# Layer-0 values by token, silu in one ScalarE operation, norm constants on VectorE, reordered loads, and a new order of the stages

## The chip, the cores and the metric

One core of one Trainium2 chip. The metric is the device time of one execution in microseconds; lower is better. The time before is the median of 3 runs.

## What is computed

The input x has 32 sequences of 32 tokens with 128 features. Two layers follow each other:

```python
# layer 0: a conditioned transformer block, 16 heads of 8 channels
cmod = silu(c) @ w_ada + b_ada                  # six vectors of 128 for each sequence
x_mod = ln(x) * (1 + scale_msa) + shift_msa
k, q, v = split(x_mod @ w_qkv, 3)
w = softmax((q / 8) @ k.T)                      # for each head, 32 x 32
x = x + gate_msa * ((w @ v) @ w_proj + b_proj)
h = gelu((ln(x) * (1 + scale_mlp) + shift_mlp) @ w_mlp1 + b_mlp1)
x = x + gate_mlp * (h @ w_mlp2 + b_mlp2)
# layer 1: graph attention in two directions d, over the first 20 tokens
self = concat(x, q or 0) @ W_self.T + b_self    # 0 where a row of x sums to 0
out = self
for d in (0, 1):
    vb = A[d] @ w_bias + b_bias                 # A: the int32 mask, or its transpose
    w = softmax(where(A[d].sum(-1) > 0, qd @ kd.T / sqrt(8), NEG) + vb)
    out = out + (w @ self[:20]) @ Wout[d] + bout[d]
x = x + relu(out)
```

## The kernel before, in words

The 1024 tokens are 8 groups of 128 (4 sequences each). TensorE (PE) computes a score unit, one group of one layer and direction, as 16 small matmuls into `ps_s` (`scores`, L699). Heads are split as 4 x 4: V and K are spread over four masked copies (`take k` on ScalarE (ACT) L761; `spread` on ACT L819 for layer 0 and L816 for layer 1). VectorE (DVE) takes the maximum (`max`, L982 or L977), the difference is formed on DVE (L993, layer 0) or GpSimd (POOL, L535, layer 1), PE transposes the result (`turn`, L711), ACT takes the exponential into PT (`exp`, L824), PE multiplies by V (`values`), and DVE divides by the sum (`recip` and `mult`). There are 24 such units, 8 of layer 0 and 16 of layer 1.

Layer 0's values are feature-major before: V is the stationary operand and PT the moving one (L727), so y comes out as features by tokens, ready for the projection. The sums come from a second product with `quad_ones` (L731), four matmuls of 128 columns, and are as wide as y: the reciprocal (L1004) covers 128x128 elements and the product is L1016. Layer 1's values are token-major: PT is stationary and 36 columns of Vz are moving, 32 of V and 4 of ones that give the sums (L736); the reciprocal (L1002) covers 128x16 and the product (L1011) broadcasts it.

At the start, ACT issues the three loads of x (L743); SP issues cols, the first third of w_ada, w_qkv and the rest of w_ada (L438 to L442), waits for x and w_ada, and then issues adj, w_rest and xT (L445 to L447). silu is exp on ACT (L745) and add, reciprocal and product on DVE (L857 to L859); then follow the products with w_ada (`cmod`, L610). The norm of layer 0 works in the chunks of `STARTS` (1, 2, 2 and 3 groups): `stats` on DVE (L838, L841), `rstd` on POOL (L463 to L476: variance plus epsilon, minus the mean, the power, and the product of the two), `apply` on DVE (L846) for chunk 0 and on ACT (L804) for the others, a transposition (`xnT`, L584), two takes on DVE (L895, L893), and then the products q, k and v (L622). From the projection (L630) on the work goes in `PIECES` of 2, 3 and 3 groups: proj, x1tok (transposed for the second norm), xn2T, four mlp1 (L640) and mlp2 (L645), then rowsum, self, q1, k1 and v1 of layer 1. `label` operations on POOL (L510 to L530) reduce the mask to the bias of layer 1.

One list, `ORDER`, written out by hand, sets the order of the stages on all engines: each engine goes through it and issues the instructions of its own stages in that order. An instruction that waits holds all that stand behind it on its engine. `BANKS` says which of four PSUM banks each product uses; PE waits until the bank's last product has been taken. `fill` stages and `WARM` are matmuls of the identity whose results nobody reads.

## Time and profile before

| | |
|---|---|
| median of 3 runs | 95.74 us (95.59 to 96.35) |
| profiled execution, its own time | 95.43 us |
| its span, first to last instruction | 93.6 us |
| instructions | 4637 |
| PE, DVE busy | 88%, 79% of the span |
| ACT, POOL busy | 67%, 68% of the span |
| TensorE clock granted | 1.00 throughout |

Busy time is the union of an engine's instructions. The execution's own time is 1.8 us longer than the span; that part lies around it. PEld is the loading of weights, which overlaps the matmuls. In the rows, x32 counts instruction records; an f32 product has two of them.

### The profile page before, as it was taken

The page shows a single profiled execution, that of the slowest core. Times are in us where ns is not written, and L with a number is a line of the kernel's source. Part 1 is how long each engine was busy: PE and PEld are TensorE (multiplying, and loading weights), DVE is VectorE, ACT ScalarE, POOL GpSimd, SP SyncE. Part 2 cuts the span into 40 slices and gives each one's busy share as a digit, 9 for nine tenths or more (in the row PEclk, how much of TensorE's full clock was granted, in tenths as well). Part 3 has the DMA queues.
Part 4 walks back from the last instruction along what each step waited for, and adds up shares of the span by engine and source line. Part 5 has one row for each costly group of instructions (what it writes and reads, how often), then busy time and mean ns, then how long its engine had stood idle before and what let it go on. Part 6 is the DMA issues. An engine that isn't in the chain of part 4 may idle for free.

```text
span 93.6 us, 4637 instructions
## 1 busy us (share of the span) xinstructions
PE 82.8 (88%) x1904; PEld 57.5 (61%) x1904; DVE 73.7 (79%) x209; ACT 63.1 (67%) x129; POOL 63.3 (68%) x117
## 2 busy tenths in 40 slices
PE   3998999977985998899998999999999999997920
PEld 3996646735653685558564676558476775776810
DVE  2598798999999879994089998746399748969990
ACT  0707999966892387338970669999954547899720
POOL 6967489995599129999655199049807399895400
PEclk9999999999999999999999999999999999999999
DMA  1939994000000000000000000000000000000033
GB/s 37 304 148 308 419 399 196 0 10 3 7 0 7 0 0 3 7 0 0 0 7 0 0 7 0 7 0 7 0 7 3 7 0 7 7 3 7 7 112 112
DMA packets 2532, 5.04 MB, mean 54 GB/s; under 512 B 336, under 2 KB 1872, under 8 KB 2256
## 3 DMA queue, kind: packets, MB, share of 16 engines
q1 hardware_dynamic: 2080, 4.23, 12.5%
q10 hardware_dynamic: 432, 0.52, 1.6%
q8 instruction: 15, 0.25, 1.0%
q14 instruction: 5, 0.04, 0.1%
HBM read 4.23 MB, written 0.52 MB: 51 GB/s over the span
## 4 chain that ended last, share of the span: by engine, by line
PE 57%; DVE 26%; issue 7%; POOL 5%; ACT 1%; DVEq 0%; POOLq 0%; ACTq 0%
PE ps_p L640 8%; PE ps_p L645 7%; PE ps_s L699 7%; PE ps_p L711 7%; DVE rden_T L1004 6%; POOL Kb L550 4%; DVE neg_max L982 4%; PE ps_s L570 4%; PE ps_p L736 3%; PE ps_p L584 3%; DVE E L993 3%; PE ps_p L665 2%; PE ps_p L570 2%; DVE tok L1021 2%; PE ps_p L654 2%
## 5 line engine op out<-in xcount | busy, mean ns | idle before, releaser
L824 ACT ACTIVATE PT<-ps_p 128x512 f32<-128x512 f32 x24 | 14.0, 598 | 5.4 <-PE ps_p L711 5.1
L535 POOL TENSOR_TENSOR E<-E,neg_max 128x320 f32<-128x320 f32 x16 | 11.5, 726 | 8.6 <-DVE neg_max L977 8.6
L711 PE MATMUL ps_p<-ident,E 128*128 128x128 f32 x96 | 14.6, 278 | 0.3 <-issue 0.3
L550 POOL TENSOR_SCALAR Kb<-k_raw,cols,head_mask 128x240 f32<-128x240 f32 (+1 forms) x24 | 12.1, 518 | 3.8 <-ACT k_raw L779 3.8
L711 PEld LDWEIGHTS ps_p<-ident,E 128*128 128x128 f32 x96 | 10.9, 141 | 2.8 <-issue 1.5
L816 ACT ACTIVATE Vz<-V_turned 20x384 f32<-20x384 f32 (+1 forms) x24 | 11.5, 483 | 0.8 <-DVE V_turned L902 0.2
L766 ACT ACTIVATE hidden<-ps_p,cols 128x384 f32<-128x384 f32 (+1 forms) x12 | 6.1, 544 | 6.5 <-PE ps_p L640 6.3
L640 PE MATMUL ps_p<-xm,w_rest_sb 128*128 128x384 f32 (+1 forms) x24 | 8.7, 470 | 1.0 <-DVE xm L893 0.9
L969 DVE TENSOR_TENSOR E<-ps_s,bias_dir 128x320 f32<-128x320 f32 x16 | 7.7, 479 | 1.8 <-PE ps_s L699 1.8
L819 ACT ACTIVATE Vz<-V_turned,quad_mask 128x256 f32<-128x256 f32 (+2 forms) x16 | 7.8, 522 | 0.0
L736 PEld LDWEIGHTS ps_p<-Vz,PT 128*32 128x32 f32 x512 | 5.7, 111 | 3.2 <-issue 1.5
L1004 DVE RECIPROCAL rden_T<-ps_p 128x128 f32<-128x128 f32 x8 | 7.6, 951 | 0.1
L977 DVE TENSOR_REDUCE neg_max<-E 128x16 f32<-128x320 f32 x16 | 7.5, 475 | 0.2
L736 PE MATMUL ps_p<-Vz,PT 128*32 128x36 f32 x512 | 7.0, 201 | 0.6 <-ACT PT L824 0.6
L645 PE MATMUL ps_p<-hidden,w_rest_sb 128*128 128x384 f32 (+1 forms) x24 | 7.4, 451 | 0.0
L520 POOL TENSOR_TENSOR label_bias<-label_bias,label_tmp 128x256 f32<-128x256 f32 x10 | 7.3, 734 | 0.0
L761 ACT ACTIVATE Kb<-ps_p,head_mask 128x256 f32<-128x256 f32 (+2 forms) x16 | 6.7, 472 | 0.7 <-PE ps_p L622 0.7
L699 PE MATMUL ps_s<-Kb,q1T 32*32 32x80 f32 x512 | 7.1, 240 | 0.1
L622 PE MATMUL ps_p<-xm,w_qkv_sb 128*128 128x256 f32 (+2 forms) x24 | 7.1, 397 | 0.0
L910 DVE SCALAR_TENSOR_TENSOR ps_p<-ps_p,cols,cmod 128x384 f32<-128x384 f32 (+1 forms) x6 | 3.4, 571 | 4.1 <-PE ps_p L645 4.1
L518 POOL TENSOR_TENSOR label_sum<-label_sum,tok 128x256 int32<-128x256 int32 x9 | 6.6, 730 | 0.0
L1002 DVE RECIPROCAL rden<-ps_p 128x16 f32<-128x16 f32 x16 | 3.7, 240 | 3.6 <-PE ps_p L736 3.6
(100 smaller groups left out, 189.5 us busy)
## 6 DMA issues: line engine op xcount, KB each, us to landing
tok<-in_adj SPq DMA_DIRECT2D x1, 1408.0 KB, 5.6
w_rest_sb<-in_w_rest SPq DMA_DIRECT2D x1, 1088.0 KB, 7.9
xT<-in_xT SPq DMA_DIRECT2D x1, 512.0 KB, 8.7
x_tok<-in_x_tok ACTq DMA_DIRECT2D x1, 320.0 KB, 3.9
w_ada_sb<-in_w_ada SPq DMA_DIRECT2D x1, 256.0 KB, 4.0
out<-x_tok SPq DMA_DIRECT2D x1, 256.0 KB, 2.7
w_qkv_sb<-in_w_qkv SPq DMA_DIRECT2D x1, 192.0 KB, 3.5
out<-x_tok SPq DMA_DIRECT2D x1, 192.0 KB, 2.1
```

The source lines that it names most:

```text
L535: pool.tensor_tensor(e, e, neg_max[:, i % 3, :].unsqueeze(2).broadcast_to([P, H, M]), ALU.add)\
L550: ins = pool.tensor_scalar(Kb1[d][:, batches(h), q, :], k_raw[:, d, 0:n, :], cols[:, R_K + d:R_K + d + 1], head_mask[:, q:q + 1], ALU.add, ...
L640: return pe.matmul(ps[:, 0:cols_n], w_mlp1_sb[:, name[2], :], xm2[:, bs, :], start=True, stop=True)
L645: ins = pe.matmul(ps[:, 0:cols_n], w_mlp2_sb[:, j, :], hidden[:, j, 0:cols_n], start=(j == js[0]), stop=(j == js[-1]))
L699: ins = pe.matmul(ps_s[QUAD * b:QUAD * b + QUAD, j, 0:HI * nk], qT[q, g * UB + b, :], Kb[q, g * UB + b, :, :], start=True, stop=True)
L711: ins = pe.transpose(ps[:, j * P:(j + 1) * P], E[:, i % 3, j * HI:(j + 1) * HI, :], ident[:, :])
L736: ins = pe.matmul(ps[QUAD * b:QUAD * b + QUAD, j * VW:(j + 1) * VW], PT[:, i % PT_RING, j, b * S:(b + 1) * S], V, start=True, stop=True)
L816: act.activation(place[rows], turned_v[rows], ACT.Copy).then_inc(v_spread, 1)
L819: act.activation(place, turned_v, ACT.Copy, scale=quad_mask[:, q:q + 1]).then_inc(v_spread, 1)
L824: act.activation(PT[:, i % PT_RING, :, :], psum_of(("turn", i))[:, :].rearrange("p (j t) -> p j t", t=P), ACT.Exp)\
L969: dve.tensor_tensor(e_of(i).rearrange("p (j i) k -> p j i k", j=HJ), ps_s[:, :, 0:HI * M].rearrange("p j (i k) -> p j i k", k=M), bias_dir ...
L1004: dve.reciprocal(rden_T[:, i, :], ps[:, P:2 * P]).then_inc(rden_ready, 1)
```

## The change

- `values` of layer 0 takes the form of layer 1: token-major, 36 columns with the sums among them. `quad_ones` and `rden_T` go. y is then by token (`y_tok`), and a new stage `yT` for each piece transposes it on PE (3 dense products, 8 transposes) and copies it out on ACT, before the projection.
- silu is one ACT operation (`Silu`), followed by an Exp of one column that nobody reads. The DVE stage `silu` is gone; what stays of it (adding 1 to the scale biases) is `scales`.
- Variance plus epsilon and minus the mean are formed on DVE at the end of `stats`, with two constants set by POOL, and DVE waits on its own aggregates first; POOL's `rstd` keeps the power and the product.
- ACT issues only the first load of x; SP issues the second after the first w_ada, and the third after w_qkv.
- `POOL_SPREADS = [1]`: the four spreads of layer 0's chunk 1 of V run on POOL.
- `WARM` is 6 and not 7, the fills are 5, 1 and 1 (before 3, 1, 1, 1 and 1), and `ORDER` and `BANKS` are new throughout. In the order, POOL clears the two halves of Vz for layer 1 after rstd of chunks 2 and 3 (before: the first at once, the second after the ones); stats of a chunk stand ahead of the takes of the chunk before it; x2tok 2 stands before values 22 and 23; and the first mlp1 comes after recip 4, mult 4 and the group 1 of `yT`.

```diff
-WARM = 7
+WARM = 6
...
-    ("zero", ("pad",)), ("masks", 0), ("zero", ("values", 1, 0)), ("stats", (0, 0)), ("silu", 0), ("stats", (0, 1)),
-    ("dense", ("cmod", 0)), ("biases", 0), ("rstd", (0, 0)), ("rstd", (0, 1)), ("apply", 0),
...
+    ("masks", 0), ("zero", ("pad",)), ("zero", ("ones", 0)), ("stats", (0, 0)), ("rstd", (0, 0)), ("scales", 0),
+    ("apply", 0), ("stats", (0, 1)), ("dense", ("cmod", 0)), ("take", (("cmod", 0), 0)), ("dense", ("xnT", 0)),
+    ("take", (("xnT", 0), 0)), ("take", (("xnT", 0), 1)), ("fill", (5, "dense", ("q", 0))), ("dense", ("q", 0)),
+    ("stats", (0, 2)), ("take", (("q", 0), 0)), ("dense", ("k", 0)), ("dense", ("cmod", 1)), ("stats", (0, 3)),
+    ("rstd", (0, 1)), ("apply", 1), ("dense", ("xnT", 1)), ("dense", ("v", 0)), ("take", (("k", 0), 3)),
...
-POOL_SPREADS = []
+POOL_SPREADS = [1]
...
-            sp.dma_start(w_qkv_sb[:, :], w_qkv).then_inc(ld["qkv"], 16)
+            for n, (g0, g1) in enumerate(X_LOADS):
+                if n == 2:
+                    sp.dma_start(w_qkv_sb[:, :], w_qkv).then_inc(ld["qkv"], 16)
+                if n:
+                    sp.dma_start(x_tok[:, g0:g1, :], x_dram[:, g0:g1, :]).then_inc(ld_x[n], 16)
...
-                by_scalar = layer == 0 and APPLY_ON[c] == "ACT"
-                pool.tensor_scalar(var_eps[:, layer, g0:g1], meanvar[:, g0:g1, 1], 1.0, LN_EPS, ALU.mult, ALU.add)\
-                    .then_inc(pool_own, 1)
-                if by_scalar:
-                    pool.tensor_scalar(neg_mean[:, g0:g1], meanvar[:, g0:g1, 0], -1.0, 0.0, ALU.mult, ALU.add)\
-                        .then_inc(pool_own, 1)
-                own_n += 1 + by_scalar
-                pool.wait_ge(pool_own, own_n)
...
+            pool.memset(eps[:, :], LN_EPS).then_inc(eps_ready, 1)
+            pool.memset(minus_one[:, :], -1.0).then_inc(eps_ready, 1)
...
+                if kind == "yT":
+                    pe.wait_ge(y_ready, max(UNITS.index((0, 0, g)) for g in range(g0, g1)) + 1)
+                    return turn_groups(ps, lambda i: y_tok[:, g0 + i, :], g1 - g0)
                 if kind == "proj":
                     pe.wait_ge(ld["rest"], 16)
-                    pe.wait_ge(y_ready, max(UNITS.index((0, 0, g)) for g in range(g0, g1)) + 1)
+                    wait_taken(pe, ("yT", h))
...
-                    if not layer:
-                        pe.wait_ge(biases_ready, 1)
-                        for b in range(UB):
-                            for j in range(HJ):
-                                pe.matmul(ps[QUAD * j:QUAD * j + QUAD, b * S:(b + 1) * S],
-                                          Vz[:, g * UB + b, 0, j, 0:HI * C], PT[:, i % PT_RING, j, b * S:(b + 1) * S],
-                                          start=True, stop=True)
-                        for j in range(HJ):
-                            ins = pe.matmul(ps[QUAD * j:QUAD * j + QUAD, P:2 * P], quad_ones[:, :, :], PT[:, i % PT_RING, j, :],
-                                            start=True, stop=True)
-                    for j in range(HJ if layer else 0):
+                    for j in range(HJ):
...
-            for n, (g0, g1) in enumerate(X_LOADS):
-                act.dma_start(x_tok[:, g0:g1, :], x_dram[:, g0:g1, :]).then_inc(ld_x[n], 16)
+            g0, g1 = X_LOADS[0]
+            act.dma_start(x_tok[:, g0:g1, :], x_dram[:, g0:g1, :]).then_inc(ld_x[0], 16)
             act.wait_ge(ld["cols"], 16)
-            act.activation(silu_t[:, 0, :], cols[:, R_COND:R_COND + B], ACT.Exp, scale=-1.0).then_inc(silu_e, 1)
+            act.activation(silu_c[:, :], cols[:, R_COND:R_COND + B], ACT.Silu).then_inc(silu_ready, 1)
+
+            act.activation(exp_first[:, :], cols[:, 0:1], ACT.Exp, scale=0.0)
...
+                if kind == "yT":
+                    return act.activation(yT[:, g0 * P:g1 * P], ps[:, 0:nb * S], ACT.Copy)
...
-                return ins
+                wait_own(ins)
+                dve.wait_ge(eps_ready, 2)
+                if by_scalar:
+                    dve.tensor_tensor(neg_mean[:, g0:g1], meanvar[:, g0:g1, 0], minus_one[:, 0:g1 - g0], ALU.mult)
+                return dve.tensor_tensor(var_eps[:, layer, g0:g1], meanvar[:, g0:g1, 1], eps[:, 0:g1 - g0], ALU.add)
...
-                dve.wait_ge(silu_e, 1)
-                wait_own(dve.tensor_tensor(silu_t[:, 1, :], silu_t[:, 0, :], ones[:, 0:B], ALU.add))
-                wait_own(dve.reciprocal(silu_t[:, 0, :], silu_t[:, 1, :]))
-                dve.tensor_tensor(silu_c[:, :], silu_t[:, 0, :], cols[:, R_COND:R_COND + B], ALU.mult)\
-                   .then_inc(silu_ready, 1)
...
-                    else:
-                        dve.reciprocal(rden_T[:, i, :], ps[:, P:2 * P]).then_inc(rden_ready, 1)
...
-                    else:
-                        dve.tensor_tensor(yT[:, g * P:(g + 1) * P], ps[:, 0:P], rden_T[:, i, :], ALU.mult)\
-                           .then_inc(y_ready, 1)
```

## Rows read from the trace of the kernel before

**Rows 1.** The page's shares: busy us and share of the span, by engine.

```profile
PE 82.8 (88%) x1904; PEld 57.5 (61%) x1904; DVE 73.7 (79%) x209; ACT 63.1 (67%) x129; POOL 63.3 (68%) x117
```

**Rows 2.** Busy time by stretch: length, then PE, PEld, DVE, ACT, POOL, clock, DMA share, GB/s.

```profile
10.00:20.00 10.00, 9.63 (x241) 5.93 (x239) 9.27 (x18) 9.54 (x27) 8.45 (x14) 1.00 0.53 218
20.00:30.00 10.00, 7.44 (x207) 4.62 (x206) 9.77 (x24) 7.10 (x13) 7.93 (x14) 1.00 0.02 4
30.00:50.00 20.00, 18.82 (x283) 12.57 (x284) 14.90 (x36) 12.53 (x22) 13.96 (x25) 1.00 0.01 2
50.00:80.00 30.00, 29.76 (x802) 19.66 (x801) 23.13 (x67) 20.90 (x40) 18.96 (x33) 1.00 0.01 4
80.00:94.00 14.00, 9.03 (x350) 7.20 (x336) 10.24 (x37) 8.76 (x18) 6.30 (x12) 1.00 0.15 42
```

**Rows 3.** The chain that ended last: its lines' shares (page), and one piece of it.

```profile
PE ps_p L640 8%; PE ps_p L645 7%; PE ps_s L699 7%; PE ps_p L711 7%; DVE rden_T L1004 6%; POOL Kb L550 4%; DVE neg_max L982 4%; PE ps_s L570 4%; PE ps_p L736 3%; PE ps_p L584 3%; DVE E L993 3%; PE ps_p L665 2%; PE ps_p L570 2%; DVE tok L1021
...
37.99 0.96 DVE rden_T L1004
```

**Rows 4.** Groups by line and form: busy us, mean ns, then idle before.

```profile
L824 ACT ACTIVATE PT<-ps_p 128x512 f32<-128x512 f32 x24 | 14.0, 598 | 5.4 <-PE ps_p L711 5.1
...
L535 POOL TENSOR_TENSOR E<-E,neg_max 128x320 f32<-128x320 f32 x16 | 11.5, 726 | 8.6 <-DVE neg_max L977 8.6
...
L1004 DVE RECIPROCAL rden_T<-ps_p 128x128 f32<-128x128 f32 x8 | 7.6, 951 | 0.1
...
L514 POOL TENSOR_SCALAR label_tmp<-tok,cols 128x256 f32<-128x256 int32 x10 | 4.8, 483 | 0.0
...
L1002 DVE RECIPROCAL rden<-ps_p 128x16 f32<-128x16 f32 x16 | 3.7, 240 | 3.6 <-PE ps_p L736 3.6
...
L563 POOL TENSOR_TENSOR xn_tok<-tok 128x128 f32<-128x128 f32 x8 | 3.7, 464 | 1.4 <-DVE tok L1011 1.4
...
L1011 DVE TENSOR_TENSOR y_tok<-ps_p,rden 128x128 f32<-128x128 f32 x8 | 2.2, 290 | 0.2
...
L783 ACT ACTIVATE tok<-ps_p 128x384 f32<-128x384 f32 x4 | 2.0, 493 | 1.5 <-PE ps_p L584 1.5
```

**Rows 5.** Timeline: the first projection and the first MLP matmul (start us, us).

```profile
20.88 0.67 PE L630 MATMUL ps_p<-yT,w_rest_sb 128*128 128x256 f32 x2 [0.67 <-ACT Kb L761]
...
28.94 0.67 PE L640 MATMUL ps_p<-xm,w_rest_sb 128*128 128x256 f32 x2 [0.47 <-DVE xm L893]
```

**Rows 6.** Timeline of PE: values of unit 0, three transposes, values of layer 1.

```profile
17.43 0.46 PE L727 MATMUL ps_p<-PT,Vz 128*32 128x32 f32 x32
17.71 0.45 PE L731 MATMUL ps_p<-PT,quad_ones 128*32 128x128 f32 x8
...
32.79 0.49 PE L584 MATMUL ps_p<-ident,x1T 128*128 128x128 f32 x3
...
79.73 0.47 PE L736 MATMUL ps_p<-Vz,PT 128*32 128x36 f32 x32
```

**Rows 7.** Timeline of the start, and the first load of w_ada (KB, us to landing).

```profile
2.13 1.28 ACT L745 ACT_TABLE_LOAD   x1 [2.13 <-issue]
...
3.42 0.23 ACT L745 ACTIVATE silu_t<-cols 128x32 f32<-128x32 f32 x1
...
4.37 0.19 DVE L859 TENSOR_TENSOR silu_c<-silu_t,cols 128x32 f32<-128x32 f32 x1
...
4.50 0.57 POOL L470 TENSOR_TENSOR rstd<-var_eps,minus_half 128x1 f32<-128x1 f32 x1
...
4.70 0.94 PE L610 MATMUL ps_p<-silu_c,w_ada_sb 128*128 128x32 f32 x4
...
w_ada_sb<-in_w_ada SPq DMA_DIRECT2D x1, 128.0 KB, 2.7
```

**Rows 8.** Timeline of the tail: the last scores and DVE's last operations.

```profile
83.20 0.66 PE L699 MATMUL ps_s<-Kb,q1T 32*32 32x80 f32 x32
...
90.43 0.69 DVE L1025 SCALAR_TENSOR_TENSOR x_tok<-tok 128x128 f32<-128x128 f32 x3
```

262 lines of the change are left out of this document (131 added, 131 removed), and 8 rows, old and new, of the table BANKS.

## The prediction, made before the changed kernel was run

> **What bounds the kernel now.** I read the page's busy shares first, then the busy time by stretch, then the chain that ended last, then single rows. The shares [rows 1] name TensorE (PE) at 88% and VectorE (DVE) at 79%, but an average hides which of them sets the pace where. By stretch [rows 2]: from 10 to 20 us DVE is busy 9.27 and ScalarE (ACT) 9.54 of 10, from 20 to 30 DVE is busy 9.77 while PE falls to 7.44, from 30 to 50 PE is busy 18.82 of 20, from 50 to 80 it is busy 29.76 of 30, and in the last 14 us neither is full. So there are four regimes: a start that waits for loads and small operations; layer 0's attention (10 to 30), paced by DVE with ACT close behind; a long middle paced by PE; and a tail that is one chain. In the DVE regime the chain [rows 3] runs over L1004, 6% of the span: a reciprocal of 128x128 elements, 951 ns each, eight of them, 7.6 us [rows 4].
>
> The marker between the second and third regime is the first MLP matmul of layer 0, at 28.94 us [rows 5]. I work out what the change does before it, after it and at the end.
>
> **Values by token.** Removed: eight reciprocals of 951 ns for eight of the kind layer 1 already has, 240 ns on 128x16: 8 x 0.71 = 5.7 us of DVE work. The mult becomes the token form of 290 ns [rows 4], as long as the feature form it replaces. On PE a unit of layer 0 takes the first 32 and then 8 matmul records from 17.43 to 18.16, 0.73 us; a token-major unit takes 0.47 [rows 6]: 8 x 0.26 = 2.1 us less. Added: eight transposes of y in three groups (a group of three takes 0.49 us [rows 6], so some 1.4 us in all), and three ACT copies out of PSUM, 0.49 us for 384 columns [rows 4]. PE thus loses 0.7 us net, and the warm-up one matmul.
>
> **Silu and the loads.** Before, silu ends on DVE: ACT's exp at 3.42, three DVE operations to 4.56, cmod's matmuls at 4.70. ACT's exp itself stood behind a table load of 1.28 us that began at 2.13, after ACT had issued its three loads of x [rows 7]. After, ACT issues one load, so the table load begins near 1.2 and silu can end near 3.0; then the weights decide, issued at 1.16 and 2.7 us on the way [rows 7], 3.9. The cmod matmuls start 0.8 us earlier. A second table load (Silu's table, then Exp's) costs 1.28 us of ACT, from 3.0 to 4.3; ACT has nothing due before its first apply near 6.8, which hides it. Without that cover it costs 1.3 us. SP now issues two loads of x between its weights, so w_qkv goes out one issue later and the last w_ada two, and with it the wait, adj, w_rest and xT behind it, by my estimate 0.8 us. I cost this at nothing: the first label operation is now placed several operations later on GpSimd (POOL), and the first projection near 21 us.
>
> **Norm constants on DVE.** POOL loses ten small operations, DVE gains ten (four plus three in layer 0's chunks, three in layer 1's pieces) and a wait on itself each time. One small DVE operation is 0.19 us [rows 7]. Before the marker stand five of the seven stats steps with eight of the ten operations: 1.5 us, or 1.3 where pairs overlap and 1.9 with the added waits, on the engine that paces there. DVE queues stats before takes; what waits for these takes is the next product on PE. It also loses a cover: DVE used to work on silu while POOL computed rstd (0.57 us, [rows 7]); now it stands about 0.6 us before the first apply.
>
> **V's chunk 1 on POOL.** POOL gains four operations on 256 columns, 0.48 us each by its nearest form, 1.9 us; ACT loses as many, some 0.5 us each by its copy of 384 columns [rows 4]. POOL's queue now holds both 2 us clearings of Vz before these, so the last spread comes near 17 us; unit 1's values are then due at about 18, as before. ACT's removed 2 us pays for the copies of y and the table load.
>
> **The sum**, against the profiled execution's 95.43 us (span 93.6):
> 1. The marker. The DVE work before it: minus four reciprocals (2.85; the fifth came after it), minus silu's three (0.73), plus 1.3 to 1.9, plus the fifth recip and two mults that the new order puts ahead (0.7), plus the wait for rstd (0.6). That is 28.9 - 3.6 + 2.6 = 27.9 as the early bound. The late bound is a walk through the new order, engine by engine with the durations of before: max 0 at about 12.1 (11.4 before), sub 1 ends at 16.2 (16.1), though by then DVE has not yet taken chunk 3's xnT or chunk 2's q and has 1 us more to do later; mults 0 and 1 end near 20.4; the first projection starts at 22.0 (20.88, [rows 5]), since y now goes through PE and ACT; max 4 ends at 24.0; the marker falls at 29.2. The walk adds 30 ns of gap per instruction and takes every wait in full, so I take a value nearer to the middle: 28.4, that is -0.5 (bounds -1.0 and +0.3).
> 2. PE's work behind the marker: three units of values less 0.26 each, plus one group of y (0.5): -0.3. The other two groups come before the marker.
> 3. PE's idle time between 30 and 80 is 1.18 + 0.24 = 1.4 us [rows 2]. DVE has 2.1 us less to do there for units 5 to 7, and two of these reciprocals were on the chain. Bounds 0 and -1.4; half, -0.7.
> 4. The tail. Before, from the last scores' start at 83.20 [rows 8] (done 83.86) to DVE's last operation at 91.12 is 7.3 us. In the new order POOL has three ya (0.46) and two subs (0.73) ahead of sub 23, 2.8 us, then sub 0.73, turn (an estimate from exp's length) and exp 0.6 each [rows 4], values 0.47, and recip, mult, ysum and relu 1.1: 6.3 us; and x2tok 2 no longer stands behind the last values. DVE has 28 operations there before and 29 after, so not all of the 1.0 is to be had: -0.7 (0 to -1.0).
>
> Sum: -0.5 - 0.3 - 0.7 - 0.7 = -2.2 us, 93.2 on this execution's own basis. It lies 0.3 us under the median 95.74 of the runs, so 93.5. All early bounds together give -3.7 (92.0), all late ones 0 (95.7).
>
> **Rivals.**
> A. The whole of the DVE work comes back: 5.7 of reciprocals plus 0.7 of silu less some 2.2 of constants is 4.2 us, 91.5. For it: L1004 is on the chain in the second regime and still at 37.99 us in the third [rows 3]. Against: from 50 to 80 PE is busy 99% of the time, and its work shrinks by under 1 us.
> By the Trainium skill, "Perfetto Trace Analysis" (Identifying the Most-Contended Engine), matmul busy time is no measure of the distance from the roofline, and the share of weight loading is the one to take. Here that is 19.66 of 30 us in the middle against 29.76 for matmuls [rows 2]; by the rule a third of the stretch is slack and a new order could use it, which speaks for A. I give it little, since PE's in-order waits appear as idle time and there are almost none.
> B. No difference: the marker stays at 29, the constants and the wait for rstd having used up the reciprocals' gain, and PE paces the rest as before with 0.3 less: 95 to 95.5. It decides if my walk is right and the middle is full.
> C. Slower: y's new path. A mult now releases the projection only over transposes on PE (0.4), a place in ACT's queue and a copy of 0.4 to 0.5. In the walk the first projection is already 1.1 us late. If that delay is not made good by the shorter DVE queue behind it, the marker falls at 30.0 and all of PE's middle with it; the two later groups can each cost the same once more when ACT holds a spread or a table load: 95.7 + 1.1 - 0.3 + 0.5 = 97.0. It decides from the point where proj 0 starts later than about 22.5.
> D. The edits don't do what they say: Silu and Exp share one table, say. It would save 1.3 us of idle ACT and nothing else; no time of its own.
>
> **How the numbers follow.** Forecast (92.3 to 94.7) 0.50; A and beyond (under 92.3) 0.18; B 0.20; C 0.12. A measurement of this kernel can tell about 1% from no change: 94.8 to 96.7 is the same. So faster 0.68, same 0.20, slower 0.12. The range 91.6 to 95.8 takes in all bounds of the sum and most of A and B.
>
> **What would show it.** L1004 gone and 24 reciprocals of about 240 ns instead of 16; DVE busy near 69.5 us, PE near 82; two table loads before 5 us; cmod's matmuls near 3.9; a DVE gap of about 0.6 us before the first apply; the first projection at 21 to 22 and the marker at 28 to 29; PE full from there; 6.5 us from the last scores to the end of DVE. The prediction is wrong if the marker comes before 27.5 or after 29.5, or if PE's idle time between 30 and 80 grows.

## The result, and where the profile after differs

In the first measurement the changed kernel took 96.39 us in the median of 20 runs (94.21 to 97.71); the kernel before, on the same chip, 95.98 (20 runs, 95.44 to 98.27). The ratio of undisturbed runs is 0.9898, 95% interval 0.9868 to 0.9927. A comparison leaves out runs more than 1.5% above the fastest of their kernel; the changed kernel's own times are spread that widely, so its ratio rests on its faster part and its median does not. Two later measurements of the same file gave 97.08 (ratio 1.0134) and 96.52 (0.996). By the medians the changed kernel is 0.4, 1.2 and 0.5% slower. So: no difference that can be told, and a spread of 3.5 us where the kernel before, but for one run of 98.27, has 1.3. The profiled execution took 96.88 us, its span is 95.1. Forecast were 93.5 us, 91.6 to 95.8.

The page's shares, by engine, of the kernel after, as in [rows 1]:

```profile
PE 82.5 (87%) x1846; PEld 58.9 (62%) x1846; DVE 69.3 (73%) x216; ACT 64.3 (68%) x129; POOL 63.7 (67%) x113
```

The work went as forecast: DVE 73.7 to 69.3 us, PE hardly less. It is the waiting that grew. Busy time by stretch, columns as in [rows 2] (length, PE, PEld, DVE, ACT, POOL, granted clock, DMA share, GB/s), the kernel after:

```profile
10.00:20.00 10.00, 8.24 (x189) 5.23 (x189) 8.33 (x20) 8.22 (x23) 9.92 (x16) 1.00 0.60 250
20.00:30.00 10.00, 8.80 (x190) 5.88 (x190) 8.03 (x24) 6.39 (x14) 6.32 (x11) 0.83 0.01 3
30.00:50.00 20.00, 19.03 (x266) 12.93 (x265) 13.08 (x37) 13.06 (x21) 16.10 (x28) 1.00 0.01 2
50.00:80.00 30.00, 29.07 (x774) 19.85 (x772) 22.17 (x66) 23.18 (x45) 19.39 (x33) 1.00 0.01 4
...
15.00:20.00 5.00, 3.37 (x136) 2.06 (x136) 3.54 (x10) 3.38 (x11) 5.00 (x9) 1.00 0.23 88
20.00:25.00 5.00, 5.00 (x52) 3.38 (x51) 3.35 (x8) 3.60 (x9) 1.99 (x4) 0.66 0.00 0
```

From 15 to 20 us PE, DVE and ACT are all a third idle; from 20 to 25 PE is busy all the time, at a granted clock of 0.66: part of that stretch ran at the lower of the two levels, 1.2 GHz. The chain that ended last and the timeline of PE say where it stood (start us, us, what), kernel after:

```profile
15.92 0.68 PE ps_p L729 x37
16.60 1.63 issue
18.22 0.39 PE ps_p L729 x21
```

```profile
18.22 0.39 PE L729 MATMUL ps_p<-Vz,PT 128*32 128x36 f32 x21 [1.63 <-issue]
...
21.44 1.06 PE L631 MATMUL ps_p<-yT,w_rest_sb 128*128 128x256 f32 x2
...
29.58 0.43 PE L641 MATMUL ps_p<-xm,w_rest_sb 128*128 128x256 f32 x1
...
83.86 0.43 PE L700 MATMUL ps_s<-Kb,q1T 32*32 32x80 f32 x32
84.23 0.58 PE L729 MATMUL ps_p<-Vz,PT 128*32 128x36 f32 x40
85.66 0.40 PE L729 MATMUL ps_p<-Vz,PT 128*32 128x36 f32 x24 [0.85 <-issue]
```

PE stops 1.63 us in the middle of a values group, after 11 of the 32 matmul records of values 1, with nothing to wait for that the profile shows. The group writes one bank and reads one PT, so no semaphore stands there; the program has its waits ahead of the group. A second such stop (0.85 us) stands behind 8 records of values 19. The two matmuls of the first projection take 1.06 us where [rows 5] has 0.67: that is the clock. Marker (first MLP matmul) 29.58, against 28.94 [rows 5].

What PE lacks at such a place is instructions. The page lists a queue that brings them, one packet of 16 KB each:

```profile
q8 instruction: 15, 0.25, 1.1%
```

I counted PE's records from the first (3692 matmuls and weight loads and 176 semaphore and drain instructions in the kernel after, 3868 in all) and set the 15 packets beside them. The stops stand behind record 448, 3520 and 3776, that is at 192 plus a multiple of 256: PE's instructions come in blocks of 256. (16 KB for 256 instructions are 64 bytes each.) With the engines free, the packet with the next block starts mostly 0.8 to 1.7 us after PE has used up a block (nine blocks in ten of the late part lie there), takes 0.9 to 1.5 us, and PE issues nothing of it sooner than 1.2 us after its end: 3.5 to 4.3 us from block to block where PE had to stop for it in the late part of the kernel after (3.85 and 4.27) and of most others. In the middle some packets start up to 0.7 us before the count says that the block is used up. The count isn't short there, since the trace has all 1846 matmul records that the order of the kernel after gives; how far ahead of PE's work a block is asked for, no run here shows. What is well shown is the other end: a stop ends 1.2 to 1.6 us after the packet's. In the kernel after PE used up record 192 at 12.29 us; the packet should have started near 13.5 and started at 16.04. The transfers of the kernel after from 12.3 to 15.8 us, and from 15.8 to 17.1 us (queue, packets, MB, share of the 16 DMA engines):

```profile
q1 hardware_dynamic: 242, 1.40, 96.4%
...
q1 hardware_dynamic: 30, 0.07, 14.3%
q8 instruction: 1, 0.02, 4.5%
```

In these 3.5 us the loads of adj, w_rest and xT fill the DMA engines, and no packet of PE's instructions moves. Before, the same packet came 2.87 us after record 192, from 14.99 to 15.93, behind the same loads. But those had been issued 0.9 us earlier, and PE reached its first values group only at 17.43 [rows 6] and record 448 at 17.75, so nothing was missed. The change delays the loads, so that the packet ends 1.05 us later, and brings record 448 forward to 16.40, and so falls into the gap.

By the Trainium skill, "DMA: Bandwidth & Descriptors" (Queues, rings and completion order), each DMA engine goes round between the queue rows it has work for, and drains a whole packet of one row, typically 9 to 17 descriptors, before it switches. The measured times from record 192 to the start are 2.0 to 5.2 us behind full queues, against 1.2 to 1.6 us where the same packet finds them empty (e2, e9, e10, e11, e14 to e16), so that the loads add 0.7 to 4 us. This neither bears the rule out nor speaks against it: if a packet of the page is an engine's whole share of w_rest, 8 of its 128 transfers at the 0.33 us that one takes in the kernel after, the wait for it is 2.7 us by my estimate, and the trace doesn't show what one packet of the page is.

### The profile page after: what moved, and what is told of

Same layout as the page of the kernel before. It is cut to its first block, busy times and chain, and to the rows that moved or that the text cites. A ratio compares the mean times of both kernels' runs of the same rounds, so it can differ in the third digit from the quotient of the medians.

```text
span 95.1 us, 4542 instructions
## 1 busy us (share of the span) xinstructions
PE 82.5 (87%) x1846; PEld 58.9 (62%) x1846; DVE 69.3 (73%) x216; ACT 64.3 (68%) x129; POOL 63.7 (67%) x113
## 4 chain that ended last, share of the span: by engine, by line
PE 64%; DVE 15%; issue 9%; POOL 5%; ACT 4%; DVEq 0%; ACTq 0%; POOLq 0%
PE ps_p L712 9%; PE ps_p L641 8%; PE ps_s L700 8%; PE ps_p L729 8%; PE ps_p L582 6%; PE ps_p L620 4%; PE ps_p L666 4%; PE ps_s L568 3%; PE ps_p L646 3%; PE ps_p L568 3%; POOL Kb L548 2%; ACT Vz L811 2%; PE ps_p L652 2%; DVE tok L1011 2%; PE ps_p L608 2%
## 5 line engine op out<-in xcount | busy, mean ns | idle before, releaser
L729 PE MATMUL ps_p<-Vz,PT 128*32 128x36 f32 x768 | 11.5, 201 | 3.4 <-issue 2.9
L729 PEld LDWEIGHTS ps_p<-Vz,PT 128*32 128x32 f32 x768 | 9.1, 111 | 7.6 <-issue 6.2
L466 POOL TENSOR_TENSOR rstd<-var_eps,minus_half 128x2 f32<-128x2 f32 (+2 forms) x7 | 5.3, 753 | 11.2 <-DVE var_eps L841 11.2
L641 PE MATMUL ps_p<-xm,w_rest_sb 128*128 128x384 f32 (+1 forms) x24 | 8.0, 464 | 0.4 <-issue 0.3
L996 DVE RECIPROCAL rden<-ps_p 128x16 f32<-128x16 f32 x24 | 5.9, 248 | 2.9 <-PE ps_p L729 2.7
L620 PE MATMUL ps_p<-xm,w_qkv_sb 128*128 128x256 f32 (+2 forms) x24 | 7.6, 427 | 0.1
L978 DVE TENSOR_REDUCE neg_max<-ps_s 128x16 f32<-128x512 f32 x8 | 5.5, 686 | 0.8 <-PE ps_s L700 0.5
```

The lines of the kernel that those rows point to most:

```text
L620: return pe.matmul(ps[:, 0:(g1 - g0) * P], w, xm[:, bs, :], start=True, stop=True)
L641: return pe.matmul(ps[:, 0:cols_n], w_mlp1_sb[:, name[2], :], xm2[:, bs, :], start=True, stop=True)
L729: ins = pe.matmul(ps[QUAD * b:QUAD * b + QUAD, j * VW:(j + 1) * VW], PT[:, i % PT_RING, j, b * S:(b + 1) * S], V, start=True, stop=True)
```

## The experiments

All were compared with the kernel before on the same chip, at the same time. "Stop" is PE's standstill behind record 448; "request" is the time from the record behind PE's 192nd to the start of the packet, since the request itself leaves no mark; marker, scores 23 (start) and DVE's end are from the profiled execution.

```
kernel             median  runs  before  ratio [95%]              request  stop  marker  sc. 23  DVE end
before              95.98   20     -       -                        2.87    0     28.94   83.20   91.12
after               96.39   20   95.98   0.9898 [0.9868, 0.9927]    3.75   1.83   29.58   83.86   93.12
e1  again           97.08    6   95.95   1.0134 [1.0100, 1.0167]    3.45   1.80   29.64   83.96   92.65
e13 again           96.52   12   96.07   0.996  [0.991, 1.001]      3.91   2.08   29.12   83.00   92.54
e2  rest late       93.63    4   95.95   0.9748 [0.9721, 0.9775]    1.30    0     26.62   80.85   89.82
e3  loads back      95.29    4   95.95   0.9897 [0.9844, 0.9951]    2.01   0.43   28.07   82.03   90.75
e4  spreads back    95.52   10   95.95   0.9963 [0.9932, 0.9994]    3.72   0.71   28.88   82.71   91.43
e5  before, late    98.24    4   96.31   1.0188 [1.0093, 1.0283]    5.17   1.69   31.03   85.65   93.78
e6  less warm-up    95.70    1   96.31     -                        0.80    0     29.64   83.27   91.90
e7  by feature     101.59    4   96.31     -                        1.86   0.18   30.15   86.72   95.45
e8  constants back  94.45    5   96.31   0.9766 [0.9668, 0.9864]    4.12   2.09   30.35   85.16   93.84
e9  hold            94.37    4   96.24   0.9842 [0.9770, 0.9914]    1.33    0     26.64   81.57   90.80
e10 hold, tail      94.89    4   96.24   0.9809 [0.9702, 0.9916]    1.57   0.18   27.03   82.18   91.13
e11 spreads back    96.02   10   96.24   0.9952 [0.9909, 0.9995]    1.20    0     28.59   83.50   93.00
e12 silu back       95.81    4   96.24     -                       -0.12    0     28.00   83.36   92.90
e14 half values     94.44    4   96.07   0.9746 [0.9677, 0.9815]    1.35   0.17   27.21   81.14   89.45
e15 pad             94.27    4   96.07   0.9790 [0.9729, 0.9850]    1.29    0     27.43   81.11   90.50
e16 constants back  94.39    4   96.07   0.9811 [0.9763, 0.9858]    1.29    0     27.07   81.35   90.89
```

A stop here is the whole gap between two instructions' issue, so it is a little longer than the idle time that the timeline prints (1.83 against 1.63).

One thing varies between these executions that the experiments don't set: when the clock first rises to 2.4 GHz. The trace's list of clock stretches begins at 5.42 us in the kernel before, 6.36 in the kernel after, 5.32 in e2, 5.50 in e9, and the filler matmuls ahead of q 0 start 0.21 us apart before that point and 0.11 us apart behind it. The windows above print 1.00 ahead of it because no stretch is on record there. In e10, e14, e15 and e16, whose programs are e9's up to that point but for e16's constants, it begins at 6.42 to 7.33, and the marker comes 0.4 to 0.8 us after e9's. Differences of that size at the marker between two profiles mean nothing by themselves.

**e1 and e13: the kernel after again.**

> The changed kernel, unaltered, for a second profile. Theory R (instruction refill): PE stops inside a group of values, at the same place in its instruction stream (43 matmul records into values 0 and 1), near 16.6 us, in every execution; its length varies, and with it the time: over 1.2 us and a granted clock of 0.5 behind it in executions above 96 us, under 0.5 us in those below 95. Rival W (ordinary wait): no stop inside a group; the lost time sits between groups, before a take or an exponential. Times 94.2 to 97.7 us as before.

> The kernel after, unchanged, with five rounds: its sign is not settled (0.9898 in the first measurement, 1.0134 in e1). Refill theory: its first refill always has adj, w_rest and xT ahead of it, so PE stops in the second values group in every run (1.2 to 1.9 us) and the time depends on whether the clock falls after it: profiles with the stop and a fallen clock end at spans of 94.6 and more, profiles with a short stop or an unfallen clock at 92.5 to 93.8. Times spread over 94.2 to 97.7; ratio to before between 0.985 and 1.015. Rival (e1 was disturbed): all within 94.2 to 95.6, ratio 0.985 to 0.990, with the stop in the trace and no fall of the clock.

The stop stands in both profiles at the same record. The two differ in the clock. In e1, as in the first profile, the clock falls behind the stop; in e13 PE stood 2.08 us and the clock stayed full (96.30 us for this execution). PE in e13 at the end of the stop, and the stretch from 20 to 25 us:

```profile
19.19 0.39 PE L729 MATMUL ps_p<-Vz,PT 128*32 128x36 f32 x21 [1.88 <-issue]
...
20.00:25.00 5.00, 4.73 (x86) 2.92 (x84) 4.53 (x13) 3.47 (x9) 2.69 (x5) 1.00 0.01 3
```

So the stop alone costs its length, and the fall is a second price that is not always paid. From the end of the stop to the marker it takes 11.36 us in the kernel after and 11.27 in e1, with the fall, and 9.93 in e13 without: 1.3 to 1.4 us. The first twenty runs show the same: the nine with a mean granted clock of 0.978 and less took 96.76 us and more, the eleven with 0.983 and more took 96.65 and less. Of e13's two expectations the first holds: the times spread from 94.81 to 97.64, with one run of 124.54.

**e2: the bulk loads later.** One line ahead of the load of w_rest:

```diff
+            sp.wait_ge(ld["adj"], 16)
             sp.dma_start(w_rest_sb[:, :, :], w_rest...
```

> The changed kernel with one wait more on SP: w_rest and xT are issued only when adj has landed (near 12.7 us instead of 7.5), so that the queues are empty for a moment near 13 us. Theory R with the bulk loads as the cause: the refill that starts at 16.0 us starts near 13 to 14, the stop near 16.6 us is gone, the clock stays at 1.00, and the time falls to 93.5 to 94.5 us and spreads by less than 0.8. If the stop stays, the bulk loads are not its cause: 94.5 to 97.5 as before. Cost: w_rest lands near 17.5, xT near 19, both before proj 0 needs them.

93.63 us, ratio 0.9748, and 3.5% under e1, with which it shared the chip. Transfers of e2 from 13.6 to 15 us, its values groups and first projection, and its stretches:

```profile
q8 instruction: 1, 0.02, 4.8%
```

```profile
16.03 0.91 PE L730 MATMUL ps_p<-Vz,PT 128*32 128x36 f32 x64
...
19.33 0.67 PE L632 MATMUL ps_p<-yT,w_rest_sb 128*128 128x256 f32 x2
```

```profile
10.00:20.00 10.00, 9.80 (x197) 6.21 (x196) 9.57 (x23) 9.22 (x26) 9.92 (x16) 1.00 0.68 260
20.00:30.00 10.00, 8.45 (x224) 5.63 (x223) 8.22 (x24) 7.72 (x16) 9.45 (x16) 1.00 0.02 5
```

The packet starts at 13.78, in the gap between adj and w_rest, whose first packets come at 13.96. Values 0 and 1 run through in 0.91 us, 64 records without a break, the clock stays full, and the marker falls at 26.62, 3.0 us earlier than after. w_rest still arrives in time, at 18.42 for a projection at 19.33. A load that nobody waited for had cost nearly 3 us by its mere presence, 1.7 by the stop and 1.3 by the clock behind it.

**e3: the loads of x on ScalarE again** (SP and ScalarE issue as before):

> The changed kernel with the loads of the kernel before: three loads of x on ACT, SP without them. The table load starts at 2.1 and not 1.2, silu ends near 3.7, cmod's matmuls start 0 to 0.3 us later than at 4.2; adj, w_rest and xT go out 0.9 us earlier. If SP's later bulk loads make the stop, it shrinks by 0.9 us (1.6 to 0.7) and the slow executions vanish: 94 to 95.5. If not, same times as the changed kernel or 0.3 more.

The bulk loads' last large packets end 0.5 us earlier (15.89 against 16.38), and the packet starts 0.4 us earlier, at 15.64. The stop shrinks to 0.43 us and the clock stays. But PE goes on behind the stop at 18.16, no earlier than after (18.22): the stop is short because the front is slower (values 0 at 17.19 against 15.85; the clock rises at 8.98 us instead of 6.36, and silu is 0.3 us later). What is gained up to the marker (28.07 against 29.58) is the clock that doesn't fall. 95.29 us beside e1's 97.08, and still 1.7 us behind e2: putting the order of issue back does not by itself take the stop away.

**e5: the same wait in the kernel before.**

> The kernel before with the same wait: w_rest and xT go out when adj has landed, near 11.8 us. In its trace the refill started at 14.4 and nothing stopped inside a group. Theory R: it has nothing to gain, 95.3 to 96.3 us (ratio 0.995 to 1.005), so the gain of 2.2 to 3 us that the wait gave the changed kernel is the changed kernel's own stop taken away. Rival L (the wait is good for any kernel, loads contend with compute): ratio under 0.985.

A miss that proved to be the best evidence. It came out 1.9% slower. Timeline of PE, e5, then its transfers from 11.7 to 16.6 us and from 16.6 to 18 us:

```profile
18.07 0.41 PE L732 MATMUL ps_p<-PT,quad_ones 128*32 128x128 f32 x5
19.90 0.41 PE L732 MATMUL ps_p<-PT,quad_ones 128*32 128x128 f32 x3 [1.42 <-issue]
```

```profile
q1 hardware_dynamic: 151, 1.14, 68.4%
...
q1 hardware_dynamic: 134, 0.47, 82.5%
q8 instruction: 1, 0.02, 4.3%
```

Here adj lands earlier, so w_rest's packets start at 13.25, just ahead of the packet of instructions (record 192 at 12.27, plus 1.2 to 1.3). That packet then starts at 17.44, 5.17 us after record 192, when 1.1 MB have passed, while xT is still on its way until 19.5, and the kernel before, which never had a stop, has one of 1.69 us behind the same record 448, and is 2.1 us later at the marker. So the stop does not come from any part of the change; it comes from the order of two requests less than half a microsecond apart.

**e8: the norms' constants on GpSimd, on top of e2.**

> e2's kernel with the norm constants back on POOL: ten small operations off DVE, ten onto POOL. The prediction's step says they cost DVE 1.3 to 1.9 us before the marker: then the time falls by 0.5 to 1 us (92.6 to 93.1). Rival: they were put on DVE because POOL's round trip is longer; back on POOL, rstd comes 0.3 us later in each chunk, and the time is the same or up to 0.8 more (93.6 to 94.4).

93.53, 94.15, 94.45, 95.5 and 97.6 us. The profiled execution is the one of 97.6, and it shows the race lost: record 192 at 12.83, w_rest's first packets at 13.53, PE's packet at 16.95, a stop of 2.09 us and the clock down behind it:

```profile
19.22 0.39 PE L738 MATMUL ps_p<-Vz,PT 128*32 128x36 f32 x21 [1.90 <-issue]
```

**e9: the load held until PE is surely past the point.**

```diff
             sp.wait_ge(ld["adj"], 16)
+            sp.wait_ge(scores_ready, 2)
             sp.dma_start(w_rest_sb[:, :, :], w_rest...
```

> The kernel after, with the load of w_rest (and xT behind it) issued only when adj has landed and PE has finished scores 1, that is, when PE has certainly passed the point (12.5 us) at which it asks for its next 256 instructions. In e2, e5 and e8 that request and the load of w_rest were issued within 0.5 us of each other: e2 (request first) had no stop, e5 and e8's profiled run (load first) had stops of 1.4 to 2.1 us in the first values group. Refill theory: here the request always wins, so the transfer of instructions starts 1.2 to 1.5 us after PE's record 192 in every run, no stop, no fall of the clock at 20 us, and all times lie as close together as those of e2: median 93.3 to 93.9, spread under 0.6 us (e8's runs spread over 4 us). Rival (e2's gain came from something else in its schedule, e8's spread from its constants on GpSimd): the times spread as those of e8, 93.5 to 97.6, and a stop shows in the trace although the transfer of instructions came early. If w_rest now lands too late (19.0 us against a first projection at 19.3) the median is up to 0.3 above e2's.

No stop, request to start 1.33 us. The median is 94.37, above the 93.3 to 93.9 expected, and the spread 1.4 us. The early part is e2's to 0.02 us at the marker (26.64). The difference lies behind the marker, most of it behind 64 us, where e9 stands 0.25 to 0.8 us at each of five block ends (records 2752, 3008, 3264, 3520, 3776), e2 1.05 at one of them and 0.11 at another. So the race was shown as the cause of the large stop, and between these two profiles the supply later on makes the difference. It isn't shown that it makes the spread of the runs: e14, which has no late stops, spreads by 2.0 us.

**e16: e8's edit on top of e9.**

> As e9, but the norms' constants computed on GpSimd again, as in e8, now with w_rest surely behind the refill. e8 had 93.53, 94.15, 94.45, 95.5 and 97.6. Refill theory: e8's slow runs were those where w_rest was issued first; here no stop at the second values group, and the spread is e9's (1.4 us): 93.7 to 95.3. The prediction's step (constants on VectorE bring the applies forward by 0.3 to 0.4 us): 0 to 0.5 us slower than e9, median 94.4 to 94.9. Rival (VectorE's added operations cost more than they bring): 0.3 to 0.8 faster than e9.

94.39 us, 93.82 to 94.76: e9's time, with none of e8's outliers. The marker is 0.43 us later than e9's, but 0.35 of that stands already at the first scores (9.20 against 8.85), where the clock had risen at 6.89 instead of 5.50. So nothing is shown of the constants on VectorE, at the marker or in the time.

**e4 and e11: the spreads of V's chunk 1 on ScalarE again** (`POOL_SPREADS = []`), on the kernel after and on e9:

> The changed kernel with chunk 1's four spreads of V back on ACT, at their places in the order. ACT gets 2 us more between 13 and 17 us, before k 2's takes. If POOL's spreads pay: values 1 and the first projection 1 to 1.5 us later, time 0.5 to 1.5 us more. If ACT has slack there, no difference. By theory R a later values group also meets an earlier refill, and the stop shrinks: then the time is no more than the changed kernel's.

> As e9, but the spreads of chunk 1 of V back on ScalarE (POOL_SPREADS empty). e4 made the same edit with the stop in place and came out 0.8% faster than the kernel after on another chip's call, which says nothing of the edit's own worth, since values 0 itself came 1.5 us late there and the stop was cut short. My theory: the spreads on GpSimd are worth what ScalarE saves in the first 20 us; without them values 0 starts 1 to 1.7 us later (17.1 to 17.7 against 16.0), the first projection 0.8 to 1.5 later, and the whole is 0.5 to 1.2 us slower than e9. Rival (ScalarE has slack there, the part is worth nothing): within 0.3 us of e9.

The same edit has opposite signs. On e9 it costs 1.7 us by the medians (by the ratios 1.1%, and their intervals just overlap): ScalarE's queue holds six spreads, the last one that values 0 needs ends at 17.93, exp 1 comes at 17.83 (15.66 in e9), and PE waits 1.5 us for values 0. Of the 2.1 us by which values 0 is later than e9's, 0.6 stands already at the first scores, where the clock rose at 7.69 instead of 5.50. Rows of e11, ScalarE and PE:

```profile
14.90 2.38 ACT L816 ACTIVATE Vz<-V_turned,quad_mask 128x256 f32<-128x256 f32 x6
...
18.03 0.91 PE L731 MATMUL ps_p<-Vz,PT 128*32 128x36 f32 x64 [1.51 <-issue]
```

On the kernel after it gains 1.6 us against e1: values 0 is 1.7 us late there too, but PE's late packet arrives meanwhile, the stop behind it is 0.71, and the clock does not fall. One delay covered the other.

**e12: silu by exponential again, on e9.**

> As e9, but silu again by an exponential on ScalarE and add, reciprocal and product on VectorE, with one table load. Theory of the prediction (the second table load is hidden, and the three small operations cost VectorE 0.5 us ahead of the first statistics): the cmod product starts 0 to 0.5 us later, the first apply 0 to 0.4 later, and the whole is 0 to 0.5 us slower than e9. Rival: the second table load was on the path, and without it the start is up to 1 us earlier, so this is faster than e9 by 0.3 to 1.0.

The medians are 1.4 us apart (95.81 and 94.37), three times what I allowed, but the runs overlap and the fastest of e12 took 94.07, so that the edit's worth in time is not shown. silu itself is 0.46 us later, and then PE's filler matmuls ahead of q 0, the same ten in both kernels, take 2.34 us instead of 1.43 (PE, first e9, then e12):

```profile
4.23 0.90 PE L610 MATMUL ps_p<-silu_c,w_ada_sb 128*128 128x32 f32 x4
5.19 1.43 PE L570 MATMUL ps_p<-ident 128*128 128x128 f32 x10
```

```profile
4.69 1.03 PE L612 MATMUL ps_p<-silu_c,w_ada_sb 128*128 128x32 f32 x4 [0.25 <-DVE silu_c L860]
5.78 2.34 PE L572 MATMUL ps_p<-ident 128*128 128x128 f32 x10
```

A late silu leaves PE idle for 0.25 us behind the warm-up, and the matmuls after it are 1.6 times as long, 234 ns each, as in the warm-up itself (12 in 2.93 us), against 143. The trace's first clock stretch begins at 9.34 us in e12 and at 5.50 in e9, and in e9 the fillers' distance falls from 0.21 to 0.11 us there, while in e12 it stays 0.21 for all ten: they ran at 1.2 GHz. The first scores are then 1.6 us late (10.43 against 8.85), 1.1 of it behind the start of cmod's matmuls. Whether the late silu is what held the clock down is not shown: with the earlier silu it rose between 4.52 and 7.69 us (thirteen profiles), with silu 0.3 and 0.46 us later at 8.98 (e3) and 9.34, but in the kernel before, with one warm-up matmul more and the same late silu, at 5.42 and in e5 at 6.80.

**e7: layer 0's values by feature again, on e2**, without y's transposes:

> e2's kernel (rest late) with layer 0's values feature-major as before: eight reciprocals of 128x128, quad_ones, no transposes of y and no copies; the order otherwise the changed kernel's, biases early. It undoes the main part. By the prediction's steps: DVE 5.7 us more, PE 0.7 more, ACT 1.3 less; if DVE paces 10 to 30 us, the marker (first mlp1 matmul, 27.5 us in e2) comes 2 to 3 us later and the time is 95.5 to 97 (ratio 1.00 +- 0.01). If PE or ACT pace there, the difference is under 1 us: 93.6 to 94.6.

101.59 us, 99.19 in the profiled execution. DVE is full again from 20 to 30 us (9.38 of 10, as in [rows 2]) and PE stands 1.36 us ahead of one scores group, of which DVE's product holds it to 28.49 and its next block of instructions, a packet that ended at 27.59, to 28.87; the marker is at 30.15, 3.5 us behind e2's. The order of the work was made for the token form, so the 5.6 us at the end (99.19 against 93.57) are not the part's own worth; that the reciprocals gate the part before the marker, they show.

**e6: a warm-up of 2 instead of 6 matmuls, on the kernel after.**

> The changed kernel with 2 warm-up matmuls instead of 6: 16 fewer instructions (8 weight loads, 8 matmuls) ahead of everything else on PE. Theory R says the stop is tied to a count of instructions: it moves from behind 43 matmul records of values 0 and 1 to behind 51, still over 0.5 us long where it was, and the second one (in values 19) moves by 8 records as well. Rival W ties it to the work: it stays behind 43 records, or goes. Time 94.5 to 97.5 us.

One run, 95.70 us, so no more than its trace can be read. Sixteen instructions fewer and a slower start, as the clock rises only at 14.56 us, and the fillers run 0.21 us apart as in e12; PE reaches record 192 only at 15.90, the packet starts 0.8 us later at 16.70, just behind the bulk loads (16.45), and there is no stop: values 0 and 1 in 0.91 us without a break. In this one run a start 3.2 us slower at the first values (19.06 against 15.85) reaches the marker at 29.64, as the kernel after does (29.58). The expected shift of the stop by 8 records could not show.

**e10: two changes of place in the tail.**

```diff
-("recip", 18), ("mult", 18), ("recip", 19), ("sub", 22), ("badd", 23), ("max", 23),
+("recip", 18), ("mult", 18), ("badd", 23), ("max", 23), ("recip", 19), ("sub", 22),
-("recip", 20), ("relu", 2), ("mult", 20),
+("recip", 20), ("mult", 20), ("relu", 2),
```

> As e9, and two changes of place on VectorE in the tail: badd 23 and max 23 ahead of recip 19 (which waits for values 19, and so for the stop of PE's instructions inside it), and mult 20 ahead of relu 2. Theory that the tail grew because the last scores' bias stood behind a reciprocal that waits for the stopped values group: badd 23 starts near 82.6 instead of 83.3, max 23 ends near 83.1 instead of 84.2, turn 23 starts right behind x2tok 2 (84.9 instead of 85.2), values 22 no longer waits 0.52 for mult 20, and the tail from scores 23 to VectorE's end goes from 9.0 us to 8.2 to 8.5: 0.5 to 0.8 us faster than e9, median 92.8 to 93.2. Rival (the tail is set by the number of instructions PE must be fed with, two refills at 3.6 us each for the last four values groups, whatever VectorE's order is): within 0.3 us of e9, with the idle time showing up as waits for issue in values 22 and 23.

From scores 23's start to DVE's end 8.95 us, e2 8.97. The median, 94.89, is above e9's where 92.8 to 93.2 was expected. The edit brought nothing that shows: the wait for mult 20 went, and a stop for instructions of 0.49 stands in its place, behind 20 records of values 22 (e10, PE):

```profile
83.98 0.40 PE L731 MATMUL ps_p<-Vz,PT 128*32 128x36 f32 x24 [0.85 <-issue]
...
87.94 0.64 PE L731 MATMUL ps_p<-Vz,PT 128*32 128x36 f32 x44 [0.49 <-issue]
```

**e15: sixteen tiny products more, at 22.8 us, on e9.**

> As e9, with 16 tiny products (64 instructions of TensorE, 0.2 us) ahead of turn 4 at 22.8 us, where it waits 0.41 us for VectorE in any case. They move every later block end 64 instructions, one values group, forward in the program. Theory: stops depend on the count of instructions alone. The stop that e2, e9 and e10 show behind the first 8 matmuls of values 19 is then behind the first 8 matmuls of values 18, and the last one (behind the first 20 matmuls of values 22 in e10) 32 matmuls earlier, ahead of values 22; the stop behind instruction 960 moves likewise. The time is within 0.5 us of e9. Rival (the stops belong to what stands there: a bank, PT, the load of a table): values 19 stops at the same matmul as before.

```profile
81.47 0.27 PE L734 MATMUL ps_p<-Vz,PT 128*32 128x36 f32 x8
82.05 0.69 PE L734 MATMUL ps_p<-Vz,PT 128*32 128x36 f32 x56 [0.31 <-issue]
...
86.05 0.26 PE L734 MATMUL ps_p<-Vz,PT 128*32 128x36 f32 x3 [1.18 <-issue]
```

64 instructions more 60 us earlier, and the stop moves from behind 8 records of values 19 to behind 8 records of values 18, one group; the last goes from values 22 to the end of values 21. The records before the stop are 3520 in both. The time is e9's (94.27). The stops belong to the count, not to the work.

**e14: half as many instructions in values 12 to 23, the same number of columns.** The weights of every second part are left out there.

> As e9, but in the values groups 12 to 23 one product of 72 columns stands in place of two of 36 (the weights of every second half are left out, so these values are not the reference's). TensorE streams the same number of columns; its instructions from 60 us on become 384 fewer of 1800, one and a half blocks of 256. Theory (from 64 us on PE is paced by its own instructions: e9's blocks of 256 there take 3.5 to 4.5 us each against 3.6 to 3.9 from one request to the next block's first instruction, and it stands 0.2 to 0.8 us at five block ends, 2.7 us in all): the stops at the block ends shrink to under 0.8 us in all, and the kernel is 1.2 to 2.5 us faster than e9, 92.0 to 93.2. Rival (the late part is set by PE's columns and by the chain of scores, bias, maximum and turn; the stops only use up slack that the next wait would show): within 0.5 us of e9, with new waits on VectorE and ScalarE where the stops were.

The stops are gone, and the median is e9's (94.44); its profiled execution is the shortest of all (93.24 us, span 91.4), others 94.19 to 95.22. PE in the tail of e14:

```profile
83.11 0.63 PE L714 MATMUL ps_p<-ident,E 128*128 128x128 f32 x4 [0.31 <-DVE tok L1012]
...
84.46 0.46 PE L731 MATMUL ps_p<-Vz,PT 128*32 128x72 f32 x16 [0.33 <-ACT PT L827]
...
86.07 0.90 PE L731 MATMUL ps_p<-Vz,PT 128*32 128x72 f32 x32 [0.24 <-DVE tok L1012]
```

Where the stops were, waits for DVE and ACT appear. From scores 23 to DVE's end it takes 8.31 us, 0.66 less than e2, 0.39 more than before. So the supply of instructions is one of two limits in the late part, with the chain over DVE close behind it. The expected gain of 1.2 to 2.5 us over e9 did not come, and the rival's 0.5 fits. The intervals of e9 and e14 overlap; that the supply costs anything in the median is not shown.

## Why the prediction was wrong

The sum's own terms, between the marks of the profiled executions:

```
                         before   after   e2      forecast   after   e2
to the marker            28.94    29.58   26.62   -0.5       +0.64   -2.32
marker to scores 23      54.26    54.28   54.23   -1.0       +0.02   -0.03
scores 23 to DVE's end    7.92     9.26    8.97   -0.7       +1.34   +1.05
sum                                               -2.2       +2.00   -1.30
```

- **The step that failed first: "I cost this at nothing"**, said of adj, w_rest and xT leaving 0.8 us later. I asked when their data is needed and not what they hold up: the packet with PE's next 256 instructions. It cost 1.8 us of standstill and, in many executions, 1.3 us more by a stretch at the lower clock behind it; e2 and e9 took it away with one or two waits (e2 3.45 us under e1 on the same chip), e5 made it in the kernel before. The later issue is a part of it and not the whole: the packet came 1.05 us later than before, and PE needed it 1.35 us earlier. The sum has no term for the supply of instructions at all, and none of the rivals had it. C had the right price by the wrong way: the first projection came at 21.44, before its point of 22.5, and y's new path showed no wait of its own.
- **Term 1, the marker (-0.5)**, was too small in itself. Without the stop it is -2.3 (e2, e9, whose clock rises when it does before; -1.5 to -1.9 in e10 and e14 to e16), past my early bound. The walk put the first projection at 22.0; it starts at 19.2 to 19.3. It charged DVE's waits in full and took values 0 from the old queue of spreads. That was off by one part above all: the spreads on GpSimd bring values 0 forward by some 1.5 us (e11), and values 1 with it, where I wrote of unit 1 "due at about 18, as before". What silu is worth stays open (e12), and the values by token are worth up to 3.5 at the marker (e7). These come one at a time and don't add up. Rival A, that more of DVE's work comes back, had the right direction for this part and only for it.
- **Terms 2 and 3, the middle (-0.3 and -0.7)**, came to zero (over all profiles of kernels with the whole order of the change, so without e7, from 0.6 less to 1.1 more). From the marker to scores 23, PE's work shrank by 0.5 us in e2 (52.44 to 51.96, from the windows between the marks), which bears out term 2. Its idle time grew from 1.8 to 2.3. "Half of 1.4 us idle" assumed that less DVE work closes PE's waits, but the waits now are for instructions, POOL's selfb (0.5) and ACT's k_raw (0.4). One stop stands right behind the marker's first record in nearly all profiles with the change (not in e6, 0.19 in e13): behind record 960 PE stands 0.63 us in the kernel after, 0.86 in e2 and 0.72 in e9, 0.05 before. The 256 instructions ahead of it now pass in 2.4 to 2.9 us (4.25 in e6), before in 3.8. Both statements of what would make the prediction wrong came true: the marker after 29.5 (29.58; 29.64 in e1, 29.12 in e13), and more idle time of PE from 30 to 80, 1.4 to 1.9 us.
- **Term 4, the tail (-0.7)**, had the wrong sign: +1.3, and +1.05 in e2. I counted DVE's operations (29) but not their time. In e2, DVE is busy 8.27 us (31 operations) from scores 23 on, 7.11 (29) before. The stop for instructions in values 19 holds recip 19 and with it bias 23 (0.85). e14 without stops still takes 0.39 more than before, so by these three profiles about two thirds of the 1.05 is the supply and one third the order; e10 shows that bias 23's place alone changes nothing.
- **Right:** L1004 gone, 24 reciprocals of 248 ns, DVE 69.3 (69.5 forecast), PE 82.5 (82), the second table load from 2.90 to 4.18 hidden, the gap of 0.62 us before the first apply, and the first projection at 21 to 22, though for another reason. cmod's matmuls came at 4.24 instead of 3.9. The engine work was forecast to 1%, the time missed by 2.9 us, since the whole of the error lies in waits.
- The middle's free third, which I had weighed for A by the Trainium skill, "Perfetto Trace Analysis" (Identifying the Most-Contended Engine), did not show: no kernel here took more than 0.6 us out of the 54 of the middle, and e2 nothing.

The version that beats both kernels is the change with the load of w_rest held back: e2 93.63, e9 94.37, e15 94.27, each some 2% under the kernel before on its chip. Of these e9 is the one that does not rest on a race. Left open: what makes the late packets of one execution late and of another not (e9 and e2 have the same instructions behind the marker); what in the loads holds the packet back, since in e5 and e8 it moves while xT is still on its way; when the clock first rises; and when it falls behind a stop, as in e1 (1.80 us), and when not, as in e13 (2.08).

## What to carry to other kernels

Straight-line code has a supply line: in this kernel every 256 instructions of TensorE are a 16 KB transfer that must be through before they are needed, and it stands behind the kernel's own bulk loads. Count the engine's instructions, semaphore instructions among them, find the marks from a stop in the trace (here 192 plus multiples of 256), and see whether a large load is issued or still running near one; if so, hold the load until the engine is past the mark, by a semaphore of that engine and not by luck. And when a kernel's times scatter by several per cent after an edit, look for a race between two requests before you judge the edit: here one edit was worth -1.6 or +1.7 us by the medians, according to who won. Compare two profiles from a common point (first scores, end of the stop, marker) and not from zero, as the clock can have risen at another time.

## What was not expected of the hardware

- A packet of TensorE's instructions is held back by the kernel's own bulk loads (402 GB/s in the 3.5 us before it in the kernel after): it starts up to 5.2 us after record 192 (e5), and 1.2 to 1.6 us after it where the queues are empty.
- From 64 us on TensorE lives at this limit in both kernels: in the kernel after a block of 256 is used up in 3.0 to 3.9 us (one in 4.9), and in the kernel before, from 68 us on, in 3.5 to 4.1; there the next block begins 1.5 to 1.8 us behind its packet's end, where 1.2 is the least that was seen; its gaps are 0.00 to 0.15 us, those of the kernel after up to 1.06.
- A float32 matmul is four records (two weight loads and two matmuls, as in x12 for a warm-up of six; a transposition is two, x4 for a turn of four), so a values group of 16 products is a quarter of a block. With small tiles the number of instructions is a cost beside the columns.
- TensorE's clock rose to 2.4 GHz at 4.5 to 7.7 us in most profiles, at 9.34 in e12 and at 14.56 in e6 with its four warm-up matmuls fewer; up to then matmuls of 128 columns start 0.21 us apart and not 0.11. A standstill of 1.8 us went twice with a stretch at 1.2 GHz behind it (the first profile and e1), one of 2.1 us once with (e8) and once without (e13), and one of 1.7 us without (e5); the stretch cost 1.1 to 1.4 us.
